# Moving stores of kept spectrum rows from the SyncE queue to the GpSimd queue in a two-stage transform and attention kernel

## The chip, the cores and the metric

The kernel runs on one core of one Trainium2 chip. The metric is the device time of one execution in microseconds (us), as the median of several runs. The kernel before has a median of 1432.56 us over 3 runs (1427.76, 1432.56 and 1433.67).

## The reference

The input is a spectrum `x` of 64 images (256 degrees, 257 orders, real and imaginary part). What is computed, cut to what matters:

```python
coeff = complex(x[..., 0], x[..., 1]) * sqrt_eig
h = irfft(einsum('nlm,mlk->nkm', coeff, pct), n=512, norm='forward')    # (64, 256, 512)
a = layernorm(h)
key = a @ K                                        # (64, 256, 512)
logits = (tanh(key @ a.T + bias) - 10000 * (1 - band)) * temperature
h = h + softmax(logits) @ a                        # a band of 12 columns
b = layernorm(h)
h = h + ffn(b)    # rows with two marks: 7 small layers, adds 2 at two one-hot places
```

All data are float32. The spectrum between the two steps has 64 images x 512 rows x 256 values: 256 orders for each of the real and the imaginary part.

## The kernel before, in words

There are two stages with a barrier of all engines between them.

**Stage 1** (`stage1_spectrum`) goes over 64 groups of 4 orders. For each group SyncE (SP) loads `xg` (512 KB) and `pg` (1 MB) into a ring of four buffers, VectorE (DVE) scales `xg` to `cg`, TensorE (PE) multiplies `cg` and `pg` into PSUM, and ScalarE (ACT) copies the result out, partition 0 to 63 holding the real part of the 64 images and 64 to 127 the imaginary part. Up to group 41 the copies go to `stage` and ACT issues their stores to the DRAM tensor `spec`. The last 22 groups are kept on chip: groups 42 to 51 in `apart` (40 orders, 40 KB in each partition), groups 52 to 63 in `hold` (48 orders). `apart` shares its bytes with tiles that stage 2 writes, its `h` among them. SP stores `apart` to `spec` behind its last loads: ten DMAs of 512 KB (line 221), counted by `apart_stored`. The spectrum of image 0 doesn't go through `spec` for the kept orders: `x0` is filled by one load from `spec`, two DMAs from `apart` (`first_apart`, line 164) and six from `hold` (`first_held`, line 158), all eight of the latter issued by ACT behind copies of groups 56, 58, 61, 62 and 63. Each reads one partition.

**Stage 2** (`stage2_blocks`) goes over the 64 images in slots -1 to 66; slots 7 to 58 are a hardware loop unrolled four times, the others are written out. Every engine runs the same list of slots, and inside a slot the order is the program's own; there is no planner. In slot i PE does the key product of image i (line 706 to 708, three products of rounded parts), the transposes of i-1, the inverse transform of image i+1 (`ps_dft`, line 742), the logits of i and the mixing of i-1. ACT copies half the key product (`keyhi`), then rounds the spectrum of image i+1 (`sphi`, line 1039), and only then copies the other half of the key product; DVE makes the remainders (`keylo`, line 1252 and 1264; `splo`, line 1260), builds `h` (line 1308 to 1327) and scales the logits with the row `rrow` (`lsc`, line 1344). GpSimd (POOL) makes the inverse roots of the variances (`rstd`, line 1478 and 1481 for the first one of a slot; I call it the first root of image i) and later in the slot the marks, the second root, and the records, which it scatters with indirect DMAs (line 1466).

SP's queue in stage 2 works strictly in order. It first waits until all ten `apart` stores have landed, then loads images 1 and 2 (`load_first`, line 616 for the rows in `spec`, line 619 for the rows that are taken from `hold` directly). In each slot it sends the first root to DRAM (line 660), waits until it has landed, and reads it back broadcast to all partitions as `rrow` (line 663). Slots 0, 1 and 2 then each issue four stores of `hold` to `spec` (`store_held`, line 632, images 4 to 63, 480 KB each). Slot 2 waits until all twelve have landed before it loads images 4, 5 and 6 (line 612). Behind that come parts of the record table (line 639) and the output of image i-2 (line 692). `x_loaded` of an image releases both `sphi` and `ps_dft` of it.

Of the kernel before, what the change touches and what calls it, by code (L numbers as in the profile page):

```python
# [18 lines left out]
NB, NLAT, MMAX, NLON = 64, 256, 257, 512  # L19
# [4 lines left out]
GM = 4  # L24
GROUPS = (MMAX - 1) // GM
# [4 lines left out]
HELD = 12  # L30
# [36 lines left out]
class OnChip:  # L67
# [3 lines left out]
    def __init__(self, nc, ctx):  # L71
# [20 lines left out]
        self.hold = sb("hold", [P, HELD * GM, NLAT])  # L92
        self.apart_stored = ctx.enter_context(nc.semaphore("apart_stored"))
        self.apart = nc.alloc_sbuf_tensor_at("apart", [P, APART * GM, NLAT], F32, offset=APART_AT)

    def add_ffn(self, nc, ctx):
# [9 lines left out]
        self.W1f = sb("W1f", [64, 4, P])  # L106


def stage1_spectrum(nc, const, xs_in, pct_in, se_in, K_in, FT_in, others, spec):


    with ExitStack() as ctx:
# [68 lines left out]
        def _(sp):  # L181
# [36 lines left out]
            m_apart = NLAT - KEPT * GM  # L218
            for j in range(APART * GM // 8):
                for c in range(2):  # L220
                    sp.dma_start(spec[0:NB, c * NLAT + m_apart + 8 * j:c * NLAT + m_apart + 8 * j + 8, :],
                                 const.apart[c * NB:c * NB + NB, 8 * j:8 * j + 8, :]).then_inc(const.apart_stored, 16)
# [87 lines left out]
        def _(act):  # L310
            def group(g, b):
# [33 lines left out]
                if isinstance(g, int) and g in (GROUPS - 8, GROUPS - 6):  # L345
                    act.wait_ge(copied, (GROUPS - HELD) * PARTS)
                    first_apart(act, (g - GROUPS + 8) // 2)
                if isinstance(g, int) and g >= GROUPS - 3:
                    m0, m1 = ((0, (HELD - 2) * GM), ((HELD - 2) * GM, (HELD - 1) * GM),
                              ((HELD - 1) * GM, HELD * GM))[g - GROUPS + 3]  # L350
                    act.wait_ge(copied, (GROUPS - HELD) * PARTS + m1 // 2)
                    for c in range(2):
                        first_held(act, c, m0, m1)
# [11 lines left out]
            groups(nc.scalar, group)  # L365
            for half in range(2):
# [3 lines left out]
def stage2_blocks(nc, const, ffn_consts, spec, recs, rs, out):  # L370


    with ExitStack() as ctx:
# [235 lines left out]
        def _(sp):  # L609
# [13 lines left out]
            sp.wait_ge(const.apart_stored, 16 * APART * GM // 4)  # L623
            for n in range(1, 3):
                load_first(n, FROM)

            def store_held(j0, j1):

                m0 = NLAT - HELD * GM
                for j in range(j0, j1):  # L630
                    for c in range(2):
                        sp.dma_start(spec[4:NB, c * NLAT + m0 + 8 * j:c * NLAT + m0 + 8 * j + 8, :],
                                     const.hold[c * NB + 4:c * NB + NB, 8 * j:8 * j + 8, :]).then_inc(hold_stored, 16)
# [23 lines left out]
            def slot(i, k, has):  # L657
# [8 lines left out]
                if isinstance(i, int) and 0 <= i < 3:  # L666
                    store_held(2 * i, 2 * i + 2)
# [970 lines left out]
```

## Time and profile before

| | us |
|---|---|
| median of 3 runs | 1432.56 |
| lowest, highest run | 1427.76, 1433.67 |
| the profiled execution | 1427.68 |
| its span | 1425.8 |
| PE busy, DVE busy, ACT busy, POOL busy | 1335.9, 928.9, 899.8, 557.0 |

The profiled execution took 1427.68 us, of which 1425.8 are the span between its first and last instruction in the trace; all times within it count from the start of the span. It lies with the fastest of the three runs. Stage 1 covers about the first 316 us, the slots of stage 2 the time from there to about 1210 us. An engine name with a q behind it (SPq, ACTq) is that engine's own queue of DMA issues.

### The profile page before, as it was taken

The page shows a single profiled execution, that of the slowest core. Times are in us where ns is not written, and L with a number is a line of the kernel's source. Part 1 is how long each engine was busy: PE and PEld are TensorE (multiplying, and loading weights), DVE is VectorE, ACT ScalarE, POOL GpSimd, SP SyncE. Part 2 cuts the span into 40 slices and gives each one's busy share as a digit, 9 for nine tenths or more (in the row PEclk, how much of TensorE's full clock was granted, in tenths as well). Part 3 has the DMA queues.
Part 4 walks back from the last instruction along what each step waited for, and adds up shares of the span by engine and source line. Part 5 has one row for each costly group of instructions (what it writes and reads, how often), then busy time and mean ns, then how long its engine had stood idle before and what let it go on. Part 6 is the DMA issues. An engine that isn't in the chain of part 4 may idle for free. (4 is left out here: it accounts for less than half of the span.)

```text
span 1425.8 us, 30434 instructions
## 1 busy us (share of the span) xinstructions
PE 1335.9 (94%) x8813; PEld 1159.2 (81%) x8813; DVE 928.9 (65%) x2026; ACT 899.8 (63%) x1956; POOL 557.0 (39%) x1394
## 2 busy tenths in 40 slices
PE   6989788969899999999999999999999989999994
PEld 4767566759799999999999999999999989555551
DVE  1222222326687887878888788887888877767772
ACT  1222222325577777777777777777777767867772
POOL 0000000000355555555555555555555546622222
PEclk9999999999999999999999999999999999999997
DMA  9999999995563333333333333333333332100000
GB/s 375 423 423 424 425 426 424 424 361 162 177 152 76 95 86 82 95 78 96 86 82 87 81 99 86 82 85 83 100 80 87 86 102 48 47 12 9 9 4 5
DMA packets 88338, 219.71 MB, mean 154 GB/s; under 512 B 20805, under 2 KB 33745, under 8 KB 75921
## 3 DMA queue, kind: packets, MB, share of 16 engines
q1 hardware_dynamic: 78265, 194.70, 42.7%
q10 hardware_dynamic: 4648, 22.89, 3.9%
q0 software_dynamic: 5376, 1.52, 0.6%
q8 instruction: 24, 0.39, 0.1%
q14 instruction: 25, 0.20, 0.1%
HBM read 147.69 MB, written 72.68 MB: 155 GB/s over the span
## 5 line engine op out<-in xcount | busy, mean ns | idle before, releaser
L708 PE MATMUL ps_k<-sphi,Glo 128*128 128x256 f32 x1024 | 292.0, 285 | 0.0
L707 PE MATMUL ps_k<-splo,Ghi 128*128 128x256 f32 x1024 | 290.7, 284 | 0.0
L706 PE MATMUL ps_k<-sphi,Ghi 128*128 128x256 f32 x1024 | 288.4, 282 | 0.0
L276 PE MATMUL s1b<-pg,cg 128*128 128x256 f32 x1024 | 241.1, 394 | 36.0 <-DVE cg L246 35.8
L276 PEld LDWEIGHTS s1b<-pg,cg 128*128 128x128 f32 x1024 | 197.5, 196 | 82.1 <-DVE cg L246 30.1
L246 DVE TENSOR_TENSOR cg<-xg,se 128x1024 f32<-128x1024 f32 x63 | 77.2, 1225 | 218.3 <-DMA pg<-in_pct_dram 206.2
L1478 POOL TENSOR_SCALAR ve<-var 128x2 f32<-128x2 f32 x64 | 13.9, 217 | 473.6 <-ACT squares L1083 473.5
L706 PEld LDWEIGHTS ps_k<-sphi,Ghi 128*128 128x128 f32 x1024 | 194.5, 190 | 2.4
L707 PEld LDWEIGHTS ps_k<-splo,Ghi 128*128 128x128 f32 x1024 | 192.9, 188 | 2.7
L708 PEld LDWEIGHTS ps_k<-sphi,Glo 128*128 128x128 f32 x1024 | 193.5, 189 | 0.0
L1466 POOL DMA_INDIRECT recs<-rec,idx x128 | 137.7, 1075 | 54.7 <-issue 54.7
L706 PE MATMUL ps_l<-sphi,keyhi 128*128 128x256 f32 x512 | 150.1, 293 | 5.2 <-DVE keylo L1264 2.3
L708 PE MATMUL ps_l<-sphi,keylo 128*128 128x256 f32 x512 | 144.7, 283 | 0.0
L707 PE MATMUL ps_l<-splo,keyhi 128*128 128x256 f32 x512 | 144.7, 283 | 0.0
L742 PE MATMUL ps_dft<-dft,xt 128*128 128x129 f32 x1008 | 130.2, 283 | 2.1 <-DMA xt<-spec 2.1
L334 ACT COPY stage<-s1b 128x512 f32<-128x512 f32 x84 | 49.2, 586 | 129.5 <-PE s1b L276 129.5
L742 PEld LDWEIGHTS ps_dft<-dft,xt 128*128 128x128 f32 x1008 | 119.7, 195 | 2.2 <-DMA xt<-spec 2.2
L1083 ACT ACTIVATE squares<-h 128x512 bf16<-128x512 f32 x128 | 79.7, 623 | 58.1 <-DVE h L1327 58.1
L706 PEld LDWEIGHTS ps_l<-sphi,keyhi 128*128 128x128 f32 x512 | 98.0, 191 | 6.2 <-issue 5.0
L706 PE MATMUL ps_av<-hhi,pThi 128*128 128x512 f32 x256 | 101.2, 395 | 1.3 <-issue 1.3
L707 PE MATMUL ps_av<-hlo,pThi 128*128 128x512 f32 x256 | 101.0, 394 | 0.0
L708 PE MATMUL ps_av<-hhi,pTlo 128*128 128x512 f32 x256 | 100.8, 394 | 0.0
(176 smaller groups left out, 3134.4 us busy)
## 6 DMA issues: line engine op xcount, KB each, us to landing
pg<-in_pct_dram SPq DMA_DIRECT2D x63, 1024.0 KB, 13.0
out_dram<-o SPq DMA_DIRECT2D x64, 512.0 KB, 2.8
xg<-in_xs_dram SPq DMA_DIRECT2D x63, 512.0 KB, 10.4
xt<-spec SPq DMA_DIRECT2D x60, 512.0 KB, 5.2
spec<-stage ACTq DMA_DIRECT2D x42, 512.0 KB, 8.3
rrow<-rs SPq DMA_DIRECT2D x64, 128.0 KB, 4.5
spec<-hold SPq DMA_DIRECT2D x12, 480.0 KB, 6.0
spec<-apart SPq DMA_DIRECT2D x10, 512.0 KB, 11.6
```

What stands on the lines that cost most here:

```text
L246: nc.vector.tensor_tensor(cg[:, b % SETS], xg[:, b], se_view(g), ALU.mult).then_inc(scaled, 1)
L276: last = nc.tensor.matmul(bank[at * PARTS + part][:, m % 2, :], cg[:, b % SETS, m * 2 + h, :], pg[:, b, m * 2 + h, :], start=(h == 0), sto ...
L334: nc.scalar.copy(to, bank[at * PARTS + j][:, :, :]).then_inc(copied, 1)
L706: nc.tensor.matmul(out_ap, whi, mhi, start=(j == 0), stop=False)
L707: nc.tensor.matmul(out_ap, whi, mlo, start=False, stop=False)
L708: last = nc.tensor.matmul(out_ap, wlo, mhi, start=False, stop=(j == n - 1))
L742: last = nc.tensor.matmul(ps_dft[t][:, cols[0]:cols[1]], x[:, src, t * P:(t + 1) * P], dft[:, cols[0]:cols[1]], start=True, stop=True)
L1083: nc.scalar.activation(squares[:, 0, t], h[:, k1, t], ACT.Square, scale=1.0 / math.sqrt(NLON), accum_out=var1[:, k1 % 2, t:t + 1]).then_in ...
L1466: nc.gpsimd.indirect_dma_start(out=recs[:, :], out_offset=bass.IndirectOffsetOnAxis(ap=idx[:, r4, t:t + 1], axis=0), in_=rec[:, r4, t, :], ...
L1478: nc.gpsimd.tensor_scalar(ve[:, 0, :], var1[:, k % 2, :], EPS, None, ALU.add).then_inc(pool_ve, 1)
```

## The change

The two parts of `apart` that stage 2 overwrites first (j = 1 and 0, four DMAs) are still stored by SP behind its last loads and counted by a semaphore of their own, `rows_stored`. The other six are issued by POOL as its first instructions in stage 2. The twelve stores of `hold` are issued by POOL too: six behind the first root of image 0, six behind that of image 1. In stage 1 both `first_apart` stand behind group 55 on ACT; five of the six `first_held` move to SP, and ACT issues the sixth behind its last copy. SP's first loads in stage 2 wait for both semaphores; DVE waits for `rows_stored` before `h` of image 0 and for `apart_stored` before `h` of image 2.

```diff
--- before.py
+++ after.py
@@ -90,6 +90,7 @@
         self.x0_loaded = ctx.enter_context(nc.semaphore("x0_loaded"))
         self.hold_at = (nc.sbuf_base + 31) // 32 * 32
         self.hold = sb("hold", [P, HELD * GM, NLAT])
+        self.rows_stored = ctx.enter_context(nc.semaphore("rows_stored"))
         self.apart_stored = ctx.enter_context(nc.semaphore("apart_stored"))
         self.apart = nc.alloc_sbuf_tensor_at("apart", [P, APART * GM, NLAT], F32, offset=APART_AT)
 
@@ -104,6 +105,14 @@
         self.iota = sb("iota", [P, 16])
         self.Wf = sb("Wf", [P, MID, WCOLS])
         self.W1f = sb("W1f", [64, 4, P])
+
+
+def store_apart(eng, spec, const, j, stored):
+
+    m0 = NLAT - KEPT * GM + 8 * j
+    for c in range(2):
+        eng.dma_start(spec[0:NB, c * NLAT + m0:c * NLAT + m0 + 8, :],
+                      const.apart[c * NB:c * NB + NB, 8 * j:8 * j + 8, :]).then_inc(stored, 16)
 
 
 def stage1_spectrum(nc, const, xs_in, pct_in, se_in, K_in, FT_in, others, spec):
@@ -215,11 +224,12 @@
                     load_half(g, g % RING1, 1)
 
             sp.wait_ge(copied, (GROUPS - HELD) * PARTS)
-            m_apart = NLAT - KEPT * GM
-            for j in range(APART * GM // 8):
-                for c in range(2):
-                    sp.dma_start(spec[0:NB, c * NLAT + m_apart + 8 * j:c * NLAT + m_apart + 8 * j + 8, :],
-                                 const.apart[c * NB:c * NB + NB, 8 * j:8 * j + 8, :]).then_inc(const.apart_stored, 16)
+            for j in (1, 0):
+                store_apart(sp, spec, const, j, const.rows_stored)
+            for m0, m1 in ((0, (HELD - 2) * GM), ((HELD - 2) * GM, (HELD - 1) * GM), ((HELD - 1) * GM, HELD * GM)):
+                sp.wait_ge(copied, (GROUPS - HELD) * PARTS + m1 // 2)
+                for c in range(2 if m1 < HELD * GM else 1):
+                    first_held(sp, c, m0, m1)
 
         @block.vector
         def _(dve):
@@ -342,15 +352,10 @@
                     for c in range(2):
                         act.dma_start(spec[:, bass.ds(g * GM + (c * NLAT - GM), 2 * GM), :],
                                       stage[c * NB:(c + 1) * NB, half]).then_inc(stored[half], 16)
-                if isinstance(g, int) and g in (GROUPS - 8, GROUPS - 6):
+                if isinstance(g, int) and g == GROUPS - 9:
                     act.wait_ge(copied, (GROUPS - HELD) * PARTS)
-                    first_apart(act, (g - GROUPS + 8) // 2)
-                if isinstance(g, int) and g >= GROUPS - 3:
-                    m0, m1 = ((0, (HELD - 2) * GM), ((HELD - 2) * GM, (HELD - 1) * GM),
-                              ((HELD - 1) * GM, HELD * GM))[g - GROUPS + 3]
-                    act.wait_ge(copied, (GROUPS - HELD) * PARTS + m1 // 2)
                     for c in range(2):
-                        first_held(act, c, m0, m1)
+                        first_apart(act, c)
                 if lead and g in KF_AFTER:
                     c = KF_AFTER[g]
                     act.wait_ge(pe_KF, c + 1)
@@ -363,6 +368,8 @@
             for dst, src in others:
                 act.dma_start(dst, src).then_inc(const_loaded, 16)
             groups(nc.scalar, group)
+            act.wait_ge(copied, GROUPS * PARTS)
+            first_held(act, 1, (HELD - 1) * GM, HELD * GM)
             for half in range(2):
                 act.wait_ge(stored[half], 32 * ((GROUPS - KEPT + 2 - 2 * half) // 4))
 
@@ -620,17 +627,10 @@
                                  const.hold[c * NB + n:c * NB + n + 1, :, :].rearrange("o (p q) w -> o p (q w)", q=2)
                                  ).then_inc(x_loaded[n], 16)
 
-            sp.wait_ge(const.apart_stored, 16 * APART * GM // 4)
+            sp.wait_ge(const.rows_stored, 64)
+            sp.wait_ge(const.apart_stored, 96)
             for n in range(1, 3):
                 load_first(n, FROM)
-
-            def store_held(j0, j1):
-
-                m0 = NLAT - HELD * GM
-                for j in range(j0, j1):
-                    for c in range(2):
-                        sp.dma_start(spec[4:NB, c * NLAT + m0 + 8 * j:c * NLAT + m0 + 8 * j + 8, :],
-                                     const.hold[c * NB + 4:c * NB + NB, 8 * j:8 * j + 8, :]).then_inc(hold_stored, 16)
 
             def empty_records(q0, q1):
 
@@ -663,8 +663,6 @@
                     sp.dma_start(rrow[:, k % 2], rs[i].unsqueeze(0).to_broadcast([P, NLAT])).then_inc(rrow_loaded[k % 2], 16)
                 if isinstance(i, int) and i == 0:
                     load_first(3, FROM)
-                if isinstance(i, int) and 0 <= i < 3:
-                    store_held(2 * i, 2 * i + 2)
                 if isinstance(i, int) and i == 2:
                     sp.wait_ge(hold_stored, 16 * HELD)
                     for n in range(2):
@@ -1315,7 +1313,9 @@
                     n, k1 = i + 1, (k + 1) % 4
                     dve.wait_ge(dve_eo, n * 4 + 4)
                     if isinstance(n, int) and n == 0:
-                        dve.wait_ge(const.apart_stored, 16 * APART * GM // 4)
+                        dve.wait_ge(const.rows_stored, 64)
+                    if isinstance(n, int) and n == 2:
+                        dve.wait_ge(const.apart_stored, 96)
                     wait(dve, act_hhi, n - 3)
                     wait(dve, act_var1, (n - 3) * 2)
                     hv = h[:, k1].rearrange("p t (s w) -> p t s w", s=2)
@@ -1468,6 +1468,14 @@
                         in_=rec[:, r4, t, :], in_offset=None, bounds_check=NB * NLAT - 1,
                         oob_is_err=False).then_inc(rec_sent[r4], 16)
 
+            def store_held(j0, j1):
+
+                m0 = NLAT - HELD * GM
+                for j in range(j0, j1):
+                    for c in range(2):
+                        pool.dma_start(spec[4:NB, c * NLAT + m0 + 8 * j:c * NLAT + m0 + 8 * j + 8, :],
+                                     const.hold[c * NB + 4:c * NB + NB, 8 * j:8 * j + 8, :]).then_inc(hold_stored, 16)
+
             def slot(i, k, has):
                 ending = isinstance(i, int) and i >= NB
                 if has(i):
@@ -1479,6 +1487,8 @@
                     pool.wait_ge(pool_ve, i + 1 + (max(i - 2, 0) if isinstance(i, int) else i - 2))
                     wait(pool, rs_written, i * 16 - 48)
                     nc.gpsimd.tensor_tensor(rstd1[:, k, :], ve[:, 0, :], mhalf[:, :], ALU.pow).then_inc(pool_rstd1, 1)
+                if isinstance(i, int) and i in (0, 1):
+                    store_held(3 * i, 3 * i + 3)
                 if has(i - 3) and not ending:
                     marks(i - 3, k + 1)
                     fill_record(i - 3, (k + 1) % 4, (k + 1) % 2)
@@ -1498,6 +1508,8 @@
                         fill_record(m, m % 4, m % 2)
                         send(m, m % 4, m % 2)
 
+            for j in range(2, APART * GM // 8):
+                store_apart(pool, spec, const, j, const.apart_stored)
             pool.wait_ge(consts_set, 8)
             pool.wait_ge(dcT_set, 1)
             slots(nc.gpsimd, slot)
```

## Rows read from the trace of the kernel before

**Rows 1.** The page: busy time of the engines.

```profile
PE 1335.9 (94%) x8813; PEld 1159.2 (81%) x8813; DVE 928.9 (65%) x2026; ACT 899.8 (63%) x1956; POOL 557.0 (39%) x1394
```

**Rows 2.** Timeline of PE, 275 to 330: start us, us, what, idle before and releaser.

```profile
297.96 14.53 PE L276 MATMUL s1b<-pg,cg 128*128 128x256 f32 x64 [1.81 <-DVE cg L246]
316.97 0.45 PE L930 MATMUL ps_l<-ident,dc 64*128 64x64 f32 x2 [4.48 <-PEq L112]
321.26 3.79 PE L742 MATMUL ps_dft<-dft,x 128*128 128x129 f32 x16 [3.85 <-DMA x<-hold]
```

**Rows 3.** Timeline of ACT and its queue, end of stage 1.

```profile
313.09 1.07 ACT L334 COPY hold<-s1b 128x512 f32<-128x512 f32 x2 [2.64 <-PE s1b L276]
314.19 1.97 ACTq L158 DMA_DIRECT2D x<-hold  x2
```

**Rows 4.** Timeline of SP's queue: stores of `apart`, first load of stage 2.

```profile
299.10 10.98 SPq L221 DMA_DIRECT2D spec<-apart  x10
321.41 0.34 SPq L616 DMA_DIRECT2D xt<-spec  x1
```

**Rows 5.** Stretches: busy us of each engine, granted clock, DMA share, GB/s.

```profile
318.00:320.00 2.00, 0.00 (x0) 0.00 (x0) 0.00 (x0) 0.00 (x0) 0.00 (x0) 0.50 0.25 106
...
388.00:390.00 2.00, 0.00 (x0) 0.00 (x0) 1.95 (x7) 1.45 (x6) 0.00 (x0) 0.98 1.07 402
```

**Rows 6.** The page: issues of the moved stores, KB each, us to landing.

```profile
spec<-hold SPq DMA_DIRECT2D x12, 480.0 KB, 6.0
spec<-apart SPq DMA_DIRECT2D x10, 512.0 KB, 11.6
```

**Rows 7.** Groups of POOL: the only DMAs that it issues in the slots.

```profile
L1466 POOL DMA_INDIRECT recs<-rec,idx x128 | 137.7, 1075 | 54.7 <-issue 54.7
```

**Rows 8.** Timeline of ACT and POOL: spectrum of image 1, first roots of images 0 and 1.

```profile
329.41 1.05 ACT L1039 CAST sphi<-xt 128x1024 fp32r<-128x1024 f32 x1
...
329.60 0.73 POOL L1481 TENSOR_TENSOR rstd<-ve,mhalf 128x2 f32<-128x2 f32 x1
...
337.06 0.71 POOL L1481 TENSOR_TENSOR rstd<-ve,mhalf 128x2 f32<-128x2 f32 x1
```

**Rows 9.** Timeline of DVE: one row a slot, images 0 to 4.

```profile
329.54 0.69 DVE L1252 TENSOR_TENSOR keylo<-ps_k,keyhi 128x512 fp32r<-128x512 f32 x1 [1.87 <-ACT keyhi L1033]
...
341.40 0.69 DVE L1252 TENSOR_TENSOR keylo<-ps_k,keyhi 128x512 fp32r<-128x512 f32 x1 [1.22 <-ACT keyhi L1033]
...
356.29 0.69 DVE L1252 TENSOR_TENSOR keylo<-ps_k,keyhi 128x512 fp32r<-128x512 f32 x1 [1.34 <-ACT keyhi L1033]
...
369.71 0.69 DVE L1252 TENSOR_TENSOR keylo<-ps_k,keyhi 128x512 fp32r<-128x512 f32 x1 [1.34 <-ACT keyhi L1033]
...
391.85 0.69 DVE L1252 TENSOR_TENSOR keylo<-ps_k,keyhi 128x512 fp32r<-128x512 f32 x1 [1.36 <-ACT keyhi L1033]
```

**Rows 10.** Timeline of DVE: the scaled logits of images 0, 1 and 3.

```profile
337.73 0.69 DVE L1344 TENSOR_TENSOR lsc<-ps_l,rrow 128x512 f32<-128x512 f32 x1 [1.40 <-DMA rrow<-rs]
...
350.97 0.69 DVE L1344 TENSOR_TENSOR lsc<-ps_l,rrow 128x512 f32<-128x512 f32 x1 [2.23 <-DMA rrow<-rs]
...
386.51 0.69 DVE L1344 TENSOR_TENSOR lsc<-ps_l,rrow 128x512 f32<-128x512 f32 x1 [4.88 <-DMA rrow<-rs]
```

**Rows 11.** Timeline of SP's queue, slots 2 and 3.

```profile
360.13 4.50 SPq L632 DMA_DIRECT2D spec<-hold  x4
369.60 1.44 SPq L612 DMA_DIRECT2D xt<-spec  x3
...
372.13 0.48 SPq L660 DMA_DIRECT2D rs<-rstd  x1
381.56 0.35 SPq L663 DMA_DIRECT2D rrow<-rs  x1
```

**Rows 12.** Timeline of ACT: the spectrum of image 4.

```profile
373.24 1.05 ACT L1039 CAST sphi<-xt 128x1024 fp32r<-128x1024 f32 x1 [3.63 <-DMA xt<-spec]
```

**Rows 13.** SP's line 663: DMA from issue to landing, minimum, median, maximum.

```profile
DMA to landing us min/median/max: 2.9/4.5/5.6
```

## The prediction

> **What bounds the kernel now.** I read the page first. PE is busy 94% of the span [rows 1], so time can only come from the places where PE stands idle or runs at half clock. PE's timeline then shows where that is near the change. It ends stage 1 at 297.96 + 14.53 = 312.49, and apart from 0.45 us it has nothing to do until 321.26, 8.8 us later, when the last pieces of x0 from hold have landed [rows 2]. The other place is found by one row per slot on DVE: keylo of images 0 to 4 starts at 329.54, 341.40, 356.29, 369.71 and 391.85, so the slots last 11.86 (no mixing yet), 14.89, 13.42 and 22.14 us [rows 9]. I take the 13.42, in which no wait on a DMA falls, for a slot that nothing holds up. The fourth is then 8.7 too long and the second 1.45.
>
> SP's queue explains the 8.7. Its last stores of hold are issued until 364.6, and it then waits until 369.60 for all twelve to have landed before it may load image 4 [rows 11]; ACT waits 3.63 us for that image [rows 12]. The root of image 3 is issued behind those three loads at 372.13, takes 9.4 us until SP can read it back at 381.56 [rows 11], and DVE waits 4.88 us for the broadcast [rows 10]. PE does nothing from 388 to 390 [rows 5]. The 1.45 is the same thing in small: a wait of 2.23 for the broadcast of image 1, whose root stood in SP's ring behind four stores [rows 10].
>
> **The change part by part.**
>
> *Stage 1 on ACT.* The last two copies end at 314.16 and two issues follow until 316.16 [rows 3]. Without the two issues ahead of them the copies can follow PE's end (312.49) closely, to about 313.4, and one issue of about 1.0 (half of 1.97) is left. Both engines issue theirs side by side, so the barrier falls near 314.4, 1.8 us earlier, and stage 2's first instruction (316.97 before [rows 2]) comes near 315.2. The two first_apart and the issues that SP takes over stand where neither queue is needed: nothing.
>
> *x0.* The ten stores of apart were issued until 310.1 and kept the DMA engines full; at 318 to 320 they are still 25% busy [rows 4, 5]. With four stores instead of ten in front, the last pieces of x0 should land about 2 to 3 us after their issue, near 317 instead of 321.26: 4.3 us earlier for the first transform.
>
> *The opening stores on POOL.* POOL has issued no direct store in the trace. From below the price of one is SP's 0.34 for a load [rows 4]; from above the six microseconds after which a held store lands, if the queue took one at a time [rows 6]. I take 1.1: it is the mean of POOL's own indirect DMA (1.075) [rows 7] and of SP's ten (10.98 / 10) [rows 4]. Six issues then run from 315.2 to 321.8; the 3.1 MB need 7.8 us at the 402 GB/s of a full stretch [rows 5], so the last data are written near 324 and have landed by 325.2 to 327.1 (before, the engines thinned out at 318 and SP was released at 321.4). SP can load image 1 only then, against 321.41 [rows 4]. How long it takes to land no row shows. It is at least the 2.9 of the shortest broadcast [rows 13] and at most 8.0, since ACT found the spectrum there at 329.41 without a wait [rows 4, 8]. I take 4.2, just under the median of a broadcast, because most of it is one plain load: 329.4 to 331.3, middle 330.4, and with the bounds 328 to 335. ACT must round this spectrum before it copies the second half of the keys, and logits of image 0 stand behind that. So the 4.3 us won for x0 end at this wait, and slot 0 comes out 330.4 - 329.4 = 1.0 us **later** than before.
>
> *The root of image 0.* POOL has it ready at 330.3 before [rows 8] and 4.3 earlier after, near 326, but SP issues it behind the six pieces of images 1 and 2, near 330 (six issues at 0.34 to 1.1 [rows 4], some 4 us), with POOL's first held stores beside them. I put its landing at 334.5 and the broadcast 4.5 us later [rows 13], 339.3 against 337.73 [rows 10]: 1.6 late, so 0.6 more on top of the 1 above. Loss at the opening: 1.6 us.
>
> *Held stores.* Six issues behind the root of image 0 take 6.6 us, to 332.6, and six behind that of image 1 (at 337.8 before [rows 8], near 339 after) end at 345.6. POOL's next work is in slot 2, a slot of 13.42 after that root, near 352: hidden. On SP three blocks of four issues go (4.5 us in slot 2 [rows 11]). The root of image 1 no longer stands behind stores of its own queue: 1.45 back. All twelve have landed near 351.6 (6.0 after the last issue [rows 6]) instead of 369.6, so images 4, 5 and 6 are loaded 18 us earlier; nobody waits for image 4, the root of image 3 finds an empty queue (2.9 at the least and 4.5 at the median for a broadcast [rows 13]), DVE's wait of 4.88 is gone and the slot takes 13.42: 8.7 back. PE's pause at 388 goes with it and is inside the 8.7.
>
> DVE's new waits cost nothing: the fourth store of SP is issued near 302.4 and lands 11.6 later [rows 4, 6], before image 0 is transformed; image 2 needs its own load anyway, and that is issued behind apart_stored.
>
> **Sum:** 1.6 lost, 1.45 and 8.7 won: 8.5 us less. The profiled execution of 1427.68 becomes 1419.2. The median of the runs stands 4.9 above the profiled execution; with the same gain it would become 1424.1. I predict between the two, 1421.5.
>
> **A rule against the change.** POOL's 128 indirect issues run beside a DVE that is 65% busy and still take 1.075 us [rows 1, 7], so I see no starving. The Trainium skill (SBUF — State Buffer, SBUF: two separate sides) says that GpSimd writes the descriptors of its DMAs itself and is locked out of the shared port while DVE runs a two-port copy; it gives some 620 ns alone and 3100 ns beside such a copy. By that figure the moved issues would cost what the first rival costs; the row speaks against it, since most of DVE's long instructions here are two-input tensor operations.
>
> **The rivals.**
>
> *POOL's issues are dear* (slower). Three batches of six and three roots stand in one queue. If one issue costs D, the broadcast of image 2 is late by 315.2 + 18 D + 2.2 + 7.4 - 364.4 = 18 D - 39.6, where 364.4 is the scaling of image 1 plus a slot (350.97 + 13.42 [rows 9, 10]), 2.2 is three roots [rows 8] and 7.4 the way of a root (2.9 and 4.5). Against the 8.7 still won later, the kernel is slower from D = 2.7, and by more than 0.5% from 3.1. At 3.5 it is 23.4 - 8.7 = 14.7 slower: 1442.4. For it: a store has many more bytes than a record. Against it: SP's ten pay 1.1 each though they stood behind a full queue. Chance 0.10.
>
> *The opening takes more.* Image 1's load runs beside the held stores and lands at 334; then PE stands still for some 8 us and falls to half clock as after stage 1 (0.50 in [rows 5]) and as in its first transform did, whose 3.79 us [rows 2] would be half as long at full clock: 1.9 lost. Gain 8.5 - 3.6 - 1.9 = 3.0: 1424.7 as profiled. For it: the stores begin later than before by design, and the engines idle between. Chance 0.22.
>
> *The opening takes nothing.* Stores issued at 0.34 and a quick landing bring image 1 by 326, and the 4.3 us stay: 10.15 + 4.3 = 14.4, 1413.3. Against it: 3.1 MB can't move faster than about 7 us. Chance 0.12.
>
> *The stores' bytes are what hurts, not the queue.* Then moving them changes little, and slots 0 to 3 stay long: a gain of about 3.6, the time of image 4's wait alone. The Trainium skill (DMA: Bandwidth & Descriptors, Issuing engines are not separate DMA queues) says that another issuing engine saves only issue time; the 9.4 us of a root that stood behind three loads [rows 11] shows more than that. Chance 0.04.
>
> **How the numbers follow.** The forecast has 0.52; its own range is a gain of 5.5 to 11, from the bounds of image 1's landing and the price of an issue. The range reaches from 1413 (nothing lost at the opening, profile's scale) to 1431 (a gain of 1.5 from the median), which leaves out the dear issues and the best ends of the third rival. A difference under 0.5% (about 7.2 us) is what a measurement of this kernel can't tell from none. Above it lie the third rival and about eight tenths of the forecast's: 0.12 + 0.43, so 0.55; slower by over 0.5% needs the dear issues: 0.09; within it lies the rest, 0.36.
>
> **What would show it.** Right: the keylo rows of images 3 and 4 stand 13.4 us apart; no wait on rrow in images 1 and 3; first transform near 317, but sphi of image 1 with a wait on xt of some 3 to 5 us, starting near 330; POOL's direct issues near 1.1 each. Wrong: issues over 2.6 us, the root of image 1 late on POOL, PE's clock at 0.50 in slot 0 or 1, or a long slot 3 that stays without stores on SP.

## The result, and the profile after

The changed kernel takes 1437.45 us (median of 17 runs, 1434.01 to 1445.64) where the kernel before took 1430.46 beside it (17 runs, 1426.05 to 1438.33). The ratio is 1.0050, 95% interval 1.0037 to 1.0063: 7.0 us **slower**, where I predicted 1421.5 and at most 1431. All ratios in this text are the record's own, taken over the runs; they can differ from the quotient of the two medians by up to about 0.1%. The profiled execution took 1438.66 us, its span is 1436.8. The page's first part, which answers to [rows 1]:

```profile
PE 1337.1 (93%) x8813; PEld 1159.3 (81%) x8813; DVE 929.8 (65%) x2026; ACT 900.7 (63%) x1956; POOL 566.0 (39%) x1412
```

Apart from POOL's eighteen issues the work is the same. What counts is where the engines stand still. PE's timeline after stage 1 (columns as in [rows 2]):

```profile
299.46 14.49 PE L286 MATMUL s1b<-pg,cg 128*128 128x256 f32 x64 [1.44 <-DVE cg L256]
...
316.32 0.45 PE L928 MATMUL ps_l<-ident,dc 64*128 64x64 f32 x2 [2.37 <-PEq L121]
316.69 3.45 PE L740 MATMUL ps_dft<-dft,x 128*128 128x129 f32 x16
...
342.00 3.37 PE L740 MATMUL ps_dft<-dft,xt 128*128 128x129 f32 x14 [16.16 <-DMA xt<-hold]
```

The first transform starts at 316.69 instead of 321.26 [rows 2], as predicted (near 317). Then PE stands still for 16.16 us until image 1 is there. POOL's and SP's queues in the same stretch:

```profile
316.82 3.36 POOL L114 DMA_DIRECT2D spec<-apart  x6 [316.38 <-POOLq L121]
...
325.39 3.20 POOL L1476 DMA_DIRECT2D spec<-hold  x6
```

```profile
329.96 0.34 SPq L623 DMA_DIRECT2D xt<-spec  x1
330.36 3.49 SPq L626 DMA_DIRECT2D xt<-hold  x2
333.90 1.58 SPq L623 DMA_DIRECT2D xt<-spec  x1
335.53 5.01 SPq L626 DMA_DIRECT2D xt<-hold  x2
341.07 0.38 SPq L660 DMA_DIRECT2D rs<-rstd  x1
344.90 0.35 SPq L663 DMA_DIRECT2D rrow<-rs  x1
```

POOL issues six stores in 3.36 us, 0.56 each. But SP, which waits until they have landed, can load image 1 only at 329.96, 13.1 us after the first issue (before: 321.41 [rows 4]). By then POOL has issued the first six held stores as well (325.39), and image 1 takes another 12 us, to 342.00. The root of image 0, which SP issues behind the loads of images 1 and 2, leaves only at 341.07. The stretches show the DMA engines 94% busy or more from 318 to 330, though at only 201 and 229 GB/s between 318 and 322, and PE at a granted clock of 0.50, its lower level, once it has stood still (columns as in [rows 5]); the transform of image 1 took 3.79 us at that level, where in the kernel before it took 1.95 at full clock:

```profile
318.00:320.00 2.00, 2.00 (x13) 2.00 (x13) 1.77 (x3) 0.37 (x1) 2.00 (x5) 0.59 0.95 201
320.00:322.00 2.00, 2.00 (x20) 2.00 (x19) 1.38 (x4) 0.37 (x1) 0.19 (x1) 1.00 0.99 229
...
326.00:328.00 2.00, 0.00 (x0) 0.00 (x0) 0.00 (x0) 0.00 (x0) 2.00 (x5) 1.00 1.01 397
334.00:336.00 2.00, 0.00 (x0) 0.00 (x0) 0.00 (x0) 0.00 (x0) 0.00 (x0) 0.50 0.96 333
344.00:346.00 2.00, 2.00 (x11) 2.00 (x10) 1.54 (x4) 0.55 (x2) 0.00 (x0) 0.50 0.00 0
```

DVE's row for each slot, against [rows 9], and the scaled logits of images 1 and 3, against [rows 10]:

```profile
324.63 0.69 DVE L1250 TENSOR_TENSOR keylo<-ps_k,keyhi 128x512 fp32r<-128x512 f32 x1 [1.88 <-ACT keyhi L1031]
...
353.35 0.69 DVE L1250 TENSOR_TENSOR keylo<-ps_k,keyhi 128x512 fp32r<-128x512 f32 x1 [1.21 <-ACT keyhi L1031]
...
369.13 0.69 DVE L1250 TENSOR_TENSOR keylo<-ps_k,keyhi 128x512 fp32r<-128x512 f32 x1 [1.33 <-ACT keyhi L1031]
...
382.56 0.69 DVE L1250 TENSOR_TENSOR keylo<-ps_k,keyhi 128x512 fp32r<-128x512 f32 x1 [1.35 <-ACT keyhi L1031]
...
396.31 0.69 DVE L1250 TENSOR_TENSOR keylo<-ps_k,keyhi 128x512 fp32r<-128x512 f32 x1 [1.66 <-ACT keyhi L1031]
```

```profile
363.81 0.69 DVE L1344 TENSOR_TENSOR lsc<-ps_l,rrow 128x512 f32<-128x512 f32 x1 [2.78 <-DMA rrow<-rs]
...
390.68 0.68 DVE L1344 TENSOR_TENSOR lsc<-ps_l,rrow 128x512 f32<-128x512 f32 x1
```

Slot 0 lasts 28.72 us instead of 11.86, slot 1 15.78 instead of 14.89, slot 3 13.75 instead of 22.14. Slot 3 gives back 8.4 us, as meant. Of the 16.9 by which slot 0 is longer, 4.9 are only its earlier start (keylo of image 0 at 324.63 for 329.54 [rows 9]); the rest is lost: keylo of image 1 comes 11.95 us later than before.

### The profile page after: what moved, and what is told of

It is laid out like the page before. It is cut to its first block and busy times, and to the rows that moved or that the text cites. A ratio compares the mean times of both kernels' runs of the same rounds, so it can differ in the third digit from the quotient of the medians.

```text
span 1436.8 us, 30436 instructions
## 1 busy us (share of the span) xinstructions
PE 1337.1 (93%) x8813; PEld 1159.3 (81%) x8813; DVE 929.8 (65%) x2026; ACT 900.7 (63%) x1956; POOL 566.0 (39%) x1412
## 5 line engine op out<-in xcount | busy, mean ns | idle before, releaser
L114 POOL DMA_DIRECT2D spec<-apart x6 | 3.4, 574 | 316.4 <-POOLq L121 316.4
L1250 DVE TENSOR_TENSOR keylo<-ps_k,keyhi 128x512 fp32r<-128x512 f32 x64 | 44.3, 692 | 87.1 <-ACT keyhi L1031 87.1
```

The source lines that it names most:

```text
L1250: nc.vector.tensor_tensor(keylo[:, 0:2, :].rearrange("p e w -> p (e w)"), ps_k[0][:, :], keyhi[:, 0:2, :].bitcast(F32).rearrange("p e w -> ...
```

## The experiments

One table holds what the traces of all kernels have in common. A slot is counted from keylo of its image to keylo of the next; "to image 1" and "to image 5" are counted from PE's end of stage 1 to keylo of that image, and "behind" is from keylo of image 63 to the end of the span. A kernel with an earlier first transform also starts slot 0 earlier, so what the opening costs is read in "to image 1" and not in the length of slot 0. Between images 5 and 63 all of them take 804.1 to 805.8.

| kernel | ratio to before, 95% | slots 0, 1, 2, 3 | to image 1 | to image 5 | behind |
|---|---|---|---|---|---|
| before (3 traces) | 1 | 11.9-12.4, 14.3-14.9, 13.4-13.9, 22.1-24.4 | 28.2-28.9 | 92.8-94.4 | 215.2-221.2 |
| changed (3 traces) | 1.0050 [1.0037, 1.0063] | 28.6-29.3, 15.6-15.8, 13.4, 13.8 | 39.0-39.5 | 95.2-95.8 | 216.6-225.3 |
| held_only | 0.9991 [0.9980, 1.0003] | 17.75, 14.41, 13.81, 13.64 | 34.7 | 90.3 | 220.5 |
| open_only | 1.0035 [1.0019, 1.0051] | 23.18, 14.92, 13.45, 19.52 | 32.9 | 94.4 | 220.8 |
| held_later | 1.0014 [1.0001, 1.0028] | 22.00, 16.07, 13.44, 16.24 | 32.7 | 92.3 | 222.9 |
| held_only_later | 0.9951 [0.9936, 0.9966] | 12.02, 15.15, 13.43, 15.65 | 27.5 | 85.2 | 217.8 |
| held_fours | 0.9967 [0.9951, 0.9982] | 15.56, 13.01, 13.71, 15.37 | 32.3 | 87.8 | 219.3 |
| open_on_sp | 1.0046 [1.0028, 1.0065] | 29.61, 16.03, 13.43, 13.75 | 39.8 | 96.4 | 220.4 |
| open_two | 0.9982 [0.9968, 0.9995] | 30.87, 13.48, 14.44, 13.99 | 45.4 | 100.7 | 219.3 |
| x0_and_later | 0.9968 [0.9955, 0.9980] | 11.96, 15.16, 13.42, 15.19 | 27.8 | 85.1 | 220.4 |
| later_spread | 0.9942 [0.9925, 0.9960] | 12.81, 15.41, 13.43, 13.45 | 29.0 | 85.5 | 214.4 |
| x0_only | 1.0016 [1.0004, 1.0028] | 12.48, 14.55, 13.43, 21.08 | 29.1 | 91.9 | 223.2 |

**Theories.** A: the stores that open the stage land late, and image 1 with them; the held stores on POOL are harmless. B: bulk stores in flight hold up every small transfer, whoever's queue they stand in, so that the held batches hurt as well where a load or a root stands beside them. C: POOL's queue is what costs.

### Held stores alone, and opening stores alone

held_only is the kernel before with one change: the held stores leave SP's slot and stand in POOL's, behind the first root.

```diff
-                if isinstance(i, int) and 0 <= i < 3:
-                    store_held(2 * i, 2 * i + 2)
...
+                if isinstance(i, int) and i in (0, 1):
+                    store_held(3 * i, 3 * i + 3)
```

> The kernel before with the twelve held stores alone moved to GpSimd (six behind each of the first two roots); stage 1, x0 and all ten apart stores stay as before. Theory A (the loss sits in the opening: six apart stores issued late, and SP's first loads waiting for them): this one gains. SP issues image 1 at 321.4 as before; the six held stores start near 330, after images 1 and 2 have landed; slot 3 is 13.5 us instead of 22.1, so about 8 to 10 us under before (1420 to 1423 against a median of 1430.5). Theory B (stores on GpSimd's queue slow the loads wherever they stand): image 2 or the broadcast of image 0 is late by several us, slots 0 and 1 grow by 5 us or more, and the sum is within 4 us of before.

Measured: 1431.02 us against 1432.44 (ratio 0.9991). POOL, then SP, then DVE in its trace:

```profile
330.68 3.40 POOL L1466 DMA_DIRECT2D spec<-hold  x6
...
338.15 3.14 POOL L1466 DMA_DIRECT2D spec<-hold  x6
```

```profile
339.31 1.55 SPq L652 DMA_DIRECT2D rs<-rstd  x1
...
353.40 0.33 SPq L655 DMA_DIRECT2D rrow<-rs  x1
```

```profile
344.00 0.69 DVE L1334 TENSOR_TENSOR lsc<-ps_l,rrow 128x512 f32<-128x512 f32 x1 [7.30 <-DMA rrow<-rs]
```

Slot 3 gives back 8.5 us (13.64 for 22.14), and slot 0 takes 5.9 of them: DVE waits 7.30 for the broadcast of image 0, which SP issued at 333.97. The root of image 1, a write of 1 KB that SP issues behind the loads of image 3 as it did before, takes 14.1 us from its issue to the moment SP can go on (339.31 to 353.40), beside POOL's stores; in the three traces of the kernel before it took 6.3 to 7.0 behind four stores of SP's own. Most of this is covered by the longer slot 0, since slot 1 lasts no longer than before (14.41). A, which forecast 1420 to 1423, is not enough; this is what B says.

open_only is the changed kernel with the held stores back on SP, four a slot in slots 0 to 2.

> The changed kernel with the twelve held stores back on SP, four in each of slots 0, 1 and 2. Theory A: image 1 is still issued near 330, but lands some 4 to 6 us later instead of 12, since no held stores run beside it: sphi of image 1 near 335. The long slot 3 (22 us) is back, so it is slower than before by 5 to 8 us (the late image) and about equal to the changed kernel or slower. Theory B: without GpSimd's held stores the opening is harmless, image 1 lands by 331, and the kernel is within 2 us of before.

Measured: 1436.49 against 1432.44 (ratio 1.0035). Slot 0 lasts 23.18, slot 3 19.52. SP's first load comes at 328.56, 13.2 us behind the first opening store, and ACT reads image 1 at 333.76, so B's forecast for this run (image 1 by 331, within 2 us of before) fails. From PE's end of stage 1 to keylo of image 1 it takes 32.9 us for 28.2 to 28.9: the opening stores alone cost 4 to 5 us, the gain for image 0 included. In the changed kernel, with the held stores beside the load, it is 39.0 to 39.5. So both theories hold a part.

### The held stores a slot later

held_later is the changed kernel, held_only_later is held_only, both with:

```diff
-                if isinstance(i, int) and i in (0, 1):
-                    store_held(3 * i, 3 * i + 3)
+                if isinstance(i, int) and i in (1, 2):
+                    store_held(3 * i - 3, 3 * i)
```

> The changed kernel with the two batches of six held stores one slot later (behind the first roots of images 1 and 2). Theory A, with its two parts: the apart stores keep SP's first load until about 330 (unchanged), but image 1 lands near 335 instead of 342, so 6 to 7 us of the changed kernel's loss go: about 3 us faster than before. If instead the held stores had no part in the 12 us that image 1 took, sphi of image 1 stays near 342 and the time stays at the changed kernel's 1437.

> The kernel before with the held stores on GpSimd behind the first roots of images 1 and 2. Theory A: like held_only, within 2 us of it: they are all landed near 365, image 4 is needed near 369; if they land after 366 slot 3 is longer than 13.5 by the excess. Theory B: slots 0 and 1 as in before, gain limited to slot 3.

Measured: held_later 1434.27 (ratio 1.0014); held_only_later 1423.93 against 1432.44 (ratio 0.9951), **faster** by 8.5 us in the medians and 7.0 by the ratio. A had both wrong, held_later as 3 us faster than before and held_only_later as within 2 us of held_only. The opening in the trace of held_later, POOL, SP, and ACT's spectrum of image 1:

```profile
315.39 3.37 POOL L114 DMA_DIRECT2D spec<-apart  x6 [314.94 <-POOLq L121]
```

```profile
328.50 0.34 SPq L623 DMA_DIRECT2D xt<-spec  x1
```

```profile
333.66 1.05 ACT L1037 CAST sphi<-xt 128x1024 fp32r<-128x1024 f32 x1 [10.44 <-DMA xt<-hold]
```

The opening stores take 13.1 us here too, with no held store in flight (14.2 in after_third, the longest). Stretches of the same kernel show how:

```profile
318.00:320.00 2.00, 2.00 (x15) 2.00 (x15) 1.01 (x3) 0.37 (x1) 0.76 (x2) 0.76 0.89 209
320.00:322.00 2.00, 2.00 (x19) 2.00 (x19) 1.37 (x3) 0.59 (x2) 0.00 (x0) 1.00 0.99 262
322.00:324.00 2.00, 2.00 (x19) 2.00 (x18) 0.69 (x1) 1.22 (x5) 0.90 (x2) 1.00 0.96 377
324.00:326.00 2.00, 0.66 (x6) 0.45 (x4) 0.00 (x0) 0.00 (x0) 0.06 (x1) 1.00 0.97 393
```

The engines are busy from the start, but move 209 and 262 GB/s and only then some 380. Image 1 then lands in 5.2 us, where it took 12.0 in the changed kernel. So the late opening is made of two parts: 13.1 for the stores themselves, and some 7 for the held stores beside the load. In held_only_later, slots 0 and 2 last 12.02 and 13.43 and slot 3 15.65: the same stores, issued by the same queue one root later, gain 7.1 us more than in held_only (1431.02 - 1423.93). That slots 0 and 1 stay as in before and the gain sits in slot 3 is what B forecast for it. The traces of the two differ by 5.1 us ahead of image 5, and by 2.7 behind keylo of image 63.

### Four held stores a slot, on POOL

```diff
-                if isinstance(i, int) and i in (0, 1):
-                    store_held(3 * i, 3 * i + 3)
+                if isinstance(i, int) and i in (0, 1, 2):
+                    store_held(2 * i, 2 * i + 2)
```

> The kernel before with the held stores on GpSimd in the groups and the slots that SP had (four behind the first root of each of images 0, 1 and 2). Only the queue is changed, not the bytes or their slots. Queue theory (what costs is that roots and loads stand behind stores in SP's own ring): roots 1 and 3 land in about 3 us, slot 3 falls from 22 to about 15, gain 7 us or more. Bytes theory (small transfers wait beside queued stores whatever queue these are in, as the root of image 1 did in held_only with 14.1 us): the roots of images 0 to 2 still take 5 to 9 us, gain under 4 us from slots 0 to 2, the rest from image 4's earlier load only.

Measured: 1427.29 against 1432.29 (ratio 0.9967). The stores have the groups and slots that SP gave them, but the move also starts them earlier, since POOL issues them right behind the root and SP did so behind its landing, the broadcast and, in slot 0, the load of image 3: at 331.29, 339.06 and 354.87 instead of 335.49, 347.81 and 360.13. So this run prices the queue and the earlier start together: slot 3 falls from 22.14 to 15.37, slot 0 grows from 11.86 to 15.56. The roots of images 1 and 3, for which the queue theory forecast about 3 us, take 10.8 and 8.8. What slot 3 gains is the earlier load of image 4: it is issued at 365.92, 6.9 us ahead of keylo of image 3, where in the kernel before it was 0.1 ahead, and ACT no longer waits for it. That agrees with the bytes theory, which allowed a gain from this load alone.

### The opening stores issued by SP, and fewer of them

open_on_sp is the changed kernel with the opening loop of POOL moved to SP, ahead of its waits in stage 2:

```diff
+            for j in range(2, APART * GM // 8):
+                store_apart(sp, spec, const, j, const.apart_stored)
...
-            for j in range(2, APART * GM // 8):
-                store_apart(pool, spec, const, j, const.apart_stored)
```

> The changed kernel with its six opening apart stores issued by SP as its first instructions of stage 2 instead of by GpSimd. Timing theory (the stores begin at about 317 instead of in stage 1, so SP's first load waits until 330, whoever issues them): SP's first load at 329 to 331 and the time within 2 us of the changed kernel's 1437. Queue theory (GpSimd's stores are slower than SP's): SP's first load comes at 326 or before and the kernel is 3 us or more faster than the changed one.

```profile
316.42 9.03 SPq L114 DMA_DIRECT2D spec<-apart  x6
331.03 0.35 SPq L623 DMA_DIRECT2D xt<-spec  x1
```

Measured: 1437.90 (ratio 1.0046), as slow as the changed kernel, and the stores take 14.6 us. C falls for the opening stores: whose queue they stand in makes no difference that shows. By what the Trainium skill (DMA: Bandwidth & Descriptors, Issuing engines are not separate DMA queues) says, another issuing engine saves only the time of issue; here the trace agrees, 3.36 us of POOL in place of 9.03 of SP and the same time for the kernel.

open_two leaves two of the stores to the opening and gives SP eight in stage 1 (DVE's two waits change as SP's do):

```diff
+            for j in (2, 3):
+                store_apart(sp, spec, const, j, const.rows_stored)
...
-            sp.wait_ge(const.rows_stored, 64)
-            sp.wait_ge(const.apart_stored, 96)
+            sp.wait_ge(const.rows_stored, 128)
+            sp.wait_ge(const.apart_stored, 32)
...
-            for j in range(2, APART * GM // 8):
+            for j in range(4, APART * GM // 8):
```

> The changed kernel with only two apart stores (j = 4) left for the opening on GpSimd; SP stores the other eight in stage 1. Timing theory: the opening's delay scales with what is left: SP's first load near 321 to 323, sphi of image 1 near 334 (the six held stores behind root 0 still run beside it), so 6 to 8 us faster than the changed kernel: about 1430. If the opening stores are not what holds SP, its first load stays near 330.

Measured: 1429.83 against 1432.29 (ratio 0.9982), 1425.92 to 1440.07; its profiled execution is at the long end of these, so the trace shows a bad case of it, with a wait of 16.9 us for the broadcast of image 0 beside six held stores. Its opening can still be read:

```profile
318.62 1.31 POOL L114 DMA_DIRECT2D spec<-apart  x2 [318.17 <-POOLq L121]
```

```profile
325.63 0.34 SPq L625 DMA_DIRECT2D xt<-spec  x1
```

Two stores take 7.0 us and six 13.1. From these two points alone I estimate 4 us that any number pays, and 1.5 us for each store of 0.52 MB.

x0_and_later keeps the changed kernel's issues of x0, gives all ten stores of apart to SP in stage 1 and the held stores to POOL behind the roots of images 1 and 2:

```diff
+            for j in (2, 3, 4):
+                store_apart(sp, spec, const, j, const.apart_stored)
...
-            for j in range(2, APART * GM // 8):
-                store_apart(pool, spec, const, j, const.apart_stored)
...
-                if isinstance(i, int) and i in (0, 1):
-                    store_held(3 * i, 3 * i + 3)
+                if isinstance(i, int) and i in (1, 2):
+                    store_held(3 * i - 3, 3 * i)
```

> The changed kernel's issues of x0 in stage 1 (two behind group 55, five on SP, one on ACT), all ten apart stores on SP in stage 1, and GpSimd's held stores behind roots 1 and 2 as in held_only_later. If the x0 part of the change is worth what I predicted for it (up to 2 us at the barrier, when no opening store follows): 1 to 3 us faster than held_only_later's 1424. If x0's pieces, now behind ten stores on SP's queue, come late: first transform at 322 or later, and 0 to 3 us slower than held_only_later.

Measured: 1427.15 against 1432.29 (ratio 0.9968). Slots 0 to 3 are those of held_only_later (11.96, 15.16, 13.42, 15.19), so what is left of slot 0's loss is gone once no store opens the stage. But it is no faster than held_only_later, although it has the x0 part on top. The trace shows why: with ten stores ahead of them again, the pieces of x0 land late, and the first transform starts at 322.14 instead of 316.69. That is the second case of what was expected of this run.

### The loads of slot 2 spread out

In held_only_later the root of image 3 still takes 8.6 us behind the loads of images 4 to 6. later_spread is that kernel, with SP loading image 4 in slot 2, images 5 and 6 in slot 3 behind the broadcast of image 3, and 7 behind them.

```diff
-                    for n in range(2):
+                    for n in range(1):
...
+                if isinstance(i, int) and i == 3:
+                    for n in range(1, 3):
+                        sp.wait_ge(pe_dft, n * 2 + 2)
...
+                        load(n + 4, n)
-                if has(i) and has(i + 4) and not (isinstance(i, int) and i < 2):
+                if has(i) and has(i + 4) and not (isinstance(i, int) and i < 3):
```

> held_only_later with SP's three loads of slot 2 spread: image 4 in slot 2, images 5 and 6 in slot 3 behind the broadcast of image 3 and ahead of image 7. If slot 3's remaining excess (15.65 against 13.45) comes from the root of image 3 standing behind three loads in SP's ring (8.6 us to land), it falls to 13.5 and the kernel is 2 us under held_only_later: about 1422. If the root is late because of the stores and loads in flight whoever's ring they are in, slot 3 stays above 15 or the excess moves to slot 4.

SP in held_only_later, then in later_spread:

```profile
362.03 1.42 SPq L612 DMA_DIRECT2D xt<-spec  x3
364.55 0.47 SPq L652 DMA_DIRECT2D rs<-rstd  x1
373.12 0.35 SPq L655 DMA_DIRECT2D rrow<-rs  x1
```

```profile
364.66 0.39 SPq L612 DMA_DIRECT2D xt<-spec  x1
366.81 0.33 SPq L652 DMA_DIRECT2D rs<-rstd  x1
371.57 0.34 SPq L655 DMA_DIRECT2D rrow<-rs  x1
```

Measured: 1420.49 against 1428.92 (ratio 0.9942), **faster than both kernels**. The root takes 4.8 us instead of 8.6 and slot 3 13.45 instead of 15.65. But to image 5 the two kernels take the same (85.5 and 85.2): slots 0, 1 and 4 are longer by 0.8, 0.3 and 0.8, and keylo of image 0 is 0.7 later. The intervals overlap as well, so it is not shown that spreading the loads gains time.

### The same kernels again, and the x0 part alone

before_again, before_third, after_again and after_third are the two kernels unchanged, for more traces of each.

> The kernel before once more, for its trace: does the stretch behind the slots (from image 63's keylo to the end, 216.1 us in the first trace, 217.8 to 222.9 in those of the variants) vary by itself? If it does, this trace has 216 to 223 and a wait of ScalarE of some 3 us in the final layers can be in it; if that belongs to the changed kernels, it is 216 again.

> The changed kernel once more, for its trace: the slots should repeat (image 0's slot 28.7 us, slot 1 15.8, slot 3 13.7), the stretch behind the slots should vary as in before_again if it varies by itself.

> A third trace of the kernel before. If the stretch behind the slots varies by itself, it may be 220 or more here though it was 216.1 and 215.2; otherwise 215 to 217 again.

> A third trace of the changed kernel. Slots as in the other two (409.7 for image 5's keylo). Behind the slots 216 to 222, by the variation that its first two traces show (221.2, 216.6).

x0_only is the kernel before with the x0 part alone: SP stores apart in the order j = 1, 0, 2, 3, 4, then issues five of the six first_held, the waits of SP and DVE for these stores are the changed kernel's, and ACT has this:

```diff
-                if isinstance(g, int) and g in (GROUPS - 8, GROUPS - 6):
+                if isinstance(g, int) and g == GROUPS - 9:
...
-                    first_apart(act, (g - GROUPS + 8) // 2)
...
+                        first_apart(act, c)
...
+            first_held(act, 1, (HELD - 1) * GM, HELD * GM)
```

> The kernel before with the x0 part of the change alone: both first_apart behind group 55, five first_held on SP behind its ten apart stores, one on ACT; the held stores stay on SP. If the x0 part costs the 3 us by which x0_and_later stood above held_only_later: 2 to 4 us above before, seen in the end of stage 1 or in the first transform. If that difference was the spread of the runs: within 1.5 us of before.

Measured: before_again 1429.75, before_third 1432.76, after_again 1432.98, after_third 1440.78; x0_only 1435.74 against 1432.78 (ratio 1.0016). PE in the trace of x0_only:

```profile
315.73 0.30 PE L940 MATMUL ps_l<-ident,dc 64*128 64x64 f32 x2 [2.37 <-PEq L121]
...
321.66 3.79 PE L752 MATMUL ps_dft<-dft,x 128*128 128x129 f32 x16 [5.63 <-DMA x<-hold]
```

Stage 2 begins 2.37 us behind PE's end of stage 1, where the three traces of before have 3.6 to 4.5. But x0 lands no earlier, and the first transform starts at 321.66 (before: 319.5 to 321.3). The moved issues bring the barrier forward; the earlier transform of the changed kernel comes from the six stores that no longer stand ahead of x0.

Slots 0 to 2 repeat within 0.7 us, slot 3 of before within 2.3. What does not repeat is the stretch behind the slots (225.3 in after_third, above the 216 to 222 that I expected), and a row of waits on ACT goes with it. After, before_third and x0_only (columns: engine, output, line, releaser, sum, count, longest):

```profile
ACT act_f L947 <- remote: 3.1, 1, 3.1
```

```profile
ACT act_f L949 <- remote: 3.1, 1, 3.1
```

```profile
ACT act_f L959 <- remote: 5.6, 4, 2.3
```

Four of the sixteen traces have no such row (before, before_again, after_again and later_spread), and they are the four shortest behind the slots: 216.1, 215.2, 216.6, 214.4. The twelve that have it take 217.8 to 225.3. The two kernels stand on both sides, so it comes and goes by itself between executions. Of the nine traces of kernels with the x0 part eight have it, of the seven without four. Whether the x0 part makes it more frequent these counts can't decide, nor do they show that the wait is what makes the stretch long.

## Why the prediction was wrong

**Stage 1 and x0: right.** First transform 316.69 for 317, 4.6 us earlier, though the stage's first instruction comes at 316.32 and not near 315.2, since PE ended stage 1 at 313.95 in this trace (299.46 + 14.49), 1.5 later than in that of before. The reason that I gave, four stores ahead of x0 instead of ten, is borne out by x0_only.

**The price of an issue on POOL: too high, and harmless.** 0.56 us for 1.1 (page of the profile: 574 ns). The dear issues of the first rival are refuted. The Trainium skill (SBUF — State Buffer, SBUF: two separate sides) gives some 3100 ns for a DMA of GpSimd that overlaps a two-port copy of DVE. None of the eighteen issues here shows such a price; whether such a copy ran beside one of them the rows don't tell.

**The landing of the opening stores: the step that failed first.** I divided 3.1 MB by the 402 GB/s of a full stretch [rows 5] and had them landed at 325.2 to 327.1, 10.0 to 11.9 us behind the first issue at 315.2. They took 13.1 to 13.2 in three kernels (14.2 in one trace, after_third). The stretches show the reason: between 318 and 322 the engines move little more than half of the 402, and in held_later they move 160 GB/s from 316 to 318. With the later start SP is released at 329.96, 3.8 us after the 326.2 in the middle of my range.

**The landing of image 1: the step that failed most.** I took 4.2 us, so 330.4. It is 5.2 with no other store in flight and 12.0 in the changed kernel, because POOL had put six held stores beside it at 325.39, right behind the root of image 0 (324.69). That is 7.8 of the 11.6 us by which image 1 is later than predicted, the release above the other 3.8. I had counted these stores as hidden since POOL had nothing else to do; they were hidden on POOL, but not in the DMA engines. The prediction even names them beside the root of image 0, and gives them no price there. The second rival had the mechanism (half clock, PE idle, image 1 late), but put it at 334 instead of 342.00 and priced it at 3.6 + 1.9. Instead of a loss of 1.6, keylo of image 1 comes 11.95 us later than before (353.35 for 341.40), 1.5 of it from a later end of stage 1. That is the term of the sum that failed: a loss of 1.6 at the opening, where 10.5 were measured.

**The broadcast of image 1: wrong sign.** Its root no longer stands behind stores of its own queue and lands in 3.7 us (351.01 to 354.69). But the broadcast that follows flies beside six stores of POOL, issued from 350.95 on, and is there only at 363.81, 9.1 us after its issue, where I took 4.5. DVE waits 2.78 for 2.23, and slot 1 is 0.9 longer instead of 1.45 shorter.

**Slot 3: right.** 8.4 back for 8.7. held_fours shows that the late landing of SP's stores, which held back the load of image 4, made most of that slot's excess: with image 4 loaded 6.9 us ahead of keylo of image 3 instead of 0.1, 6.8 of it are gone. It can't tell whether the queue or the earlier start does that. later_spread shows the rest of it, three loads ahead of a root.

**The bytes hurt, not the queue.** I gave this rival 0.04 as a statement about slot 3, where the measured gain of 8.4 is far above its 3.6. For slot 0 it is true: held_only, held_fours and open_on_sp show it, and in slot 1 the late broadcast. I had set up queue and bytes as alternatives, where the slots show both.

**Sum.** From start to image 5 the three traces of each kernel come to 405.31, 406.90, 405.45 (mean 405.9) and 409.79, 409.67, 408.62 (mean 409.4): 3.5 us slower. The medians differ by 7.0. The rest lies behind the slots, where the means are 217.5 and 221.0. This matches in size, but that stretch alone varies by 6 to 9 us between traces of one kernel. x0_only, whose slots are in sum not longer than before's, is 0.16% slower by the ratio (2.3 us of 1432.78; 3.0 in the medians), and x0_and_later, which has held_only_later's slots, came out at 0.9968 where that one had 0.9951 (the two intervals overlap). Both point to a cost of the x0 part of some 2 us outside the slots. Over all sixteen traces PE ends stage 1 at 313.4 on the mean in the nine with the x0 part and at 312.6 in the seven without, and the stretch behind the slots has means of 221.1 and 217.8; both differences are smaller than what a group varies in itself. By what way an order of issues at 300 to 316 us could act there is **not settled**, and with it half of the measured 7.0.

## What to carry to other kernels

An engine with an idle queue is no reason to issue bulk stores: ask what small or urgent transfer will be in flight beside them, and start the stores behind it. Here the same twelve stores on the same queue are worth 0.1% behind the roots of images 0 and 1, which is not clear of nothing, and 0.5% behind those of 1 and 2. And price a transfer that an engine waits for by the landing of its last byte in a stretch of the same kind, not by bytes over the bandwidth of any full stretch.

## What the runs showed of the hardware

Six stores of 512 KB, alone in flight, kept the DMA engines 89 and 99% busy in the stretches from 318 to 322 of held_later but moved only 209 and 262 GB/s there, and some 380 only behind that; why the rate starts low is not shown. A root's write of 1 KB took up to 14.1 us beside stores of another queue (held_only), where in the three traces of the kernel before it took 9.7 at the most; a broadcast of 128 KB took 9.1 beside six stores in the changed kernel, for a median of 4.5. POOL issued a direct store of 0.5 MB in 0.56 us. SP took 1.5 each (9.03 / 6) for the same six at the opening, but 0.62 each (2.48 / 4) for the four that it issued in stage 1 of the changed kernel; what sets its price is not shown. And the stretch behind the slots varies by 6.0 us between the traces of before and by 8.7 between those of the changed kernel; the longer ones have waits on ACT whose releaser the profile can only call "remote".
